# Quadrant matmuls, contiguous PSUM copies and six early expert units in a metaformer block

## The reference, cut to what matters

```python
x_dct = einsum('bchw,kw->bchk', x, MW); x_dct = einsum('bchw,kh->bckw', x_dct, MH)   # 2D DCT of each 64x64 plane
x_tri = windows of 8x8 frequencies, [4, 64, 64, 16]
q, k  = l2norm(split(x_tri @ Wq)), l2norm(split(x_tri @ Wk));  v = split(x_tri @ Wv)
attn  = softmax(einsum('bnhdm,bnhem->bnhde', q, k) * rescale)                        # channel attention, 4 heads
x_low = (attn @ v) @ proj_w + proj_b
h1    = gelu(conv3x3_depthwise(gelu(conv1x1(x_dct))))
x_conv = h1 + x_dct
x_high = gelu(conv1x1(x_conv)) + x_conv
mixed  = coef * x_low + (1 - coef) * x_high + x_dct       # with a weight per frequency
x1     = x + inverse 2D DCT(mixed)
out    = x1 + sum over 8 experts of gate_e * (gelu(layernorm(x1) @ W1_e + b1_e) @ W2_e + b2_e)   # gates: top 2 of 8
```

## Time and profile before

| | us |
|---|---|
| median of three executions (228.82 to 233.05) | 229.17 |
| span of the profiled execution, first to last instruction | 227.4 |
| median less span | 1.8 |

### The profile page before, as it was taken

How to read it: one execution, slowest core, us unless ns; L and a number is a source line. 1 busy time by engine, 2 the same in 40 slices (tenths; PEclk the granted TensorE clock), 3 DMA queues, 4 the chain that set the end, 5 groups by cost and what they waited for, 6 DMA issues and landing times.

```text
span 227.4 us, 4913 instructions
## 1 busy us (share of the span) xinstructions
PE 206.7 (91%) x2096; PEld 113.6 (50%) x2096; DVE 123.8 (54%) x232; ACT 128.1 (56%) x207; POOL 47.0 (21%) x50
## 2 busy tenths in 40 slices
PE   7699788999976898988899799999999999999993
PEld 3395667566334577963524244444444444444430
DVE  0582055659949977999731633554334553334555
ACT  2256942035338553669685387666786666786640
POOL 5560393040069992030400000000000000000000
PEclk9979999999999999999699999999999999999998
DMA  6990000000000000000005953260804508063001
GB/s 219 294 265 14 0 3 6 3 0 7 0 0 4 0 3 0 3 0 0 3 0 164 220 128 69 82 151 0 184 3 108 122 4 184 0 150 84 0 0 46
DMA packets 6596, 14.35 MB, mean 63 GB/s; under 512 B 2736, under 2 KB 4144, under 8 KB 5680
## 3 DMA queue, kind: packets, MB, share of 16 engines
q1 hardware_dynamic: 6576, 14.06, 24.7%
HBM read 12.87 MB, written 1.18 MB: 62 GB/s over the span
## 4 chain that ended last, share of the span: by engine, by line
PE 68%; ACT 9%; DMA 7%; POOL 6%; DVE 6%; SPq 1%; issue 1%; POOLq 1%; DVEq 0%
PE psum L710 22%; PE psum L694 21%; PE psum L538 7%; DMA xs<-in_x 3%; DMA wide<-gate_store 2%; PE psum L512 2%; POOL place L920 2%; ACT place L747 2%; PE psum L634 2%; PE psum L548 2%; PE psum L424 2%; POOL place L926 2%; ACT hid L861 1%; POOL place L919 1%; PE psum L557 1%
## 5 line engine op out<-in xcount | busy, mean ns | idle before, releaser
L694 PE MATMUL psum<-tok,w1s 128*64 128x512 f16 x512 | 60.8, 383 | 1.3 <-ACT hid L861 0.8
L1160 DVE SCALAR_TENSOR_TENSOR term<-psum,sm,wide 128x512 f32<-128x512 f32 x32 | 24.0, 750 | 62.1 <-PE psum L710 51.6
L861 ACT ACTIVATE hid<-psum,b1p 128x512 f32<-128x512 f32 x64 | 38.2, 701 | 16.7 <-PE psum L694 16.3
L694 PEld LDWEIGHTS psum<-tok,w1s 128*64 128x64 f16 x512 | 28.7, 110 | 35.9 <-issue 9.1
L861 ACT ACTIVATE w1f<-psum,b1p 128x512 f32<-128x512 f32 x32 | 19.6, 688 | 17.1 <-PE psum L694 17.0
L710 PE MATMUL psum<-hid,w 128*64 128x512 f32 x128 | 28.9, 593 | 0.0
L1165 DVE TENSOR_TENSOR x<-x,term 128x512 f32<-128x512 f32 x32 | 22.1, 692 | 1.1
L861 ACT ACTIVATE w1g<-psum,b1p 128x512 f32<-128x512 f32 x32 | 19.7, 714 | 0.2
L710 PEld LDWEIGHTS psum<-hid,w 128*64 128x64 f32 x128 | 9.1, 137 | 15.1 <-issue 9.4
L710 PE MATMUL psum<-w1g,w 128*64 128x512 f32 x64 | 15.1, 594 | 1.4 <-DVE term L1160 1.4
L538 PE MATMUL psum<-h_pad,tap_bd 64*64 64x512 f32 x144 | 15.9, 589 | 0.0
(11 more groups left out here) (147 smaller groups left out, 295.4 us busy)
## 6 DMA issues: line engine op xcount, KB each, us to landing
wide<-gate_store SPq DMA_DIRECT2D x14, 512.0 KB, 6.4
xs<-in_x SPq DMA_DIRECT2D x2, 512.0 KB, 5.6
w1f<-in_W SPq DMA_DIRECT2D x2, 512.0 KB, 10.0
block_out<-x SPq DMA_DIRECT2D x4, 256.0 KB, 6.4
wide<-gate_store SPq DMA_DIRECT2D x2, 384.0 KB, 5.1
...
```

The lines of the kernel that those rows point to most:

```text
L694: mm = pe.matmul(h_bank(n)[side * H:(side + 1) * H, :], w1s[:, part, e, k * P + side * H:k * P + (side + 1) * H], tok[:, pair, half, b, :] ...
L861: act.activation(hid_of[u % 4][:, t, :], h_bank(n), ACT.Gelu, bias=b1p[:, e * KT + k:e * KT + k + 1]).then_inc(gelu_ready, 1)
L1160: dve.scalar_tensor_tensor(term[:, u % 2, :], y_bank(u), b2t[:, e:e + 1], gate_b[part][:, e % (E // 2), :], ALU.add, ALU.mult).then_inc(te ...
```

## The change

- **Quadrants.** Every 128x128 matmul of the DCTs, of `tokens`, and of the router becomes four 64x64 matmuls, one for each quadrant of the array (`quarters()` lists 32 of them for a stage), and the constants shrink to one 64x64 matrix. The transposes become 64x64 matmuls with an identity (`half_ident`).
- **Contiguous copies.** The copies from PSUM no longer rearrange. `dct_over_w` and `windows` write PSUM with a stride of 8 elements instead; `to_frequencies` and `inverse_over_kh` read their stationary operand from SBUF with a stride (8 and 16 elements).
- **Six shared copies.** For dw, xd, xt, yt, back and half ACT copies bank 0 and DVE bank 1 (`other_dw` and so on, L1032 to 1062 after). A stage now signals once, at its end, instead of once per bank.
- **POOL.** `high` has two operations per bank (L974, 975 after). A new stage `rest_ahead` (L967, 968 after) makes x_conv * (1 - coef) + x_dct, two operations per bank, before h2 is there. The constant 1 - coef moves from DVE to POOL.
- **Units.** Six units are upped early, in twelve half units at turns of their own (`UPS`), two downs and their additions come early too (`DOWNS`, `ADDS`); all later rounds stand behind turn 1000.
- **Order.** The table has new numbers for nearly all stages; the input of pair 1 is loaded ahead of the larger constants; `biases` moves ahead in DVE's order; the gates of pair 0 go out early, and gate rows are stored in pieces of 64.

```diff
-    "join": (2, 3), "high": (4, 5), "gram_matrices": (10, 16), ...
+    "join": (2, 4), "rest_ahead": (3, 6), "high": (5, 7), "gram_matrices": (12, 15), ...
...
-AHEAD = 2
+SHARED = {"dw": (1, 1), "xd": (1, 1), "xt": (1, 1), "yt": (1, 1), "back": (1, 1), "half": (1, 1)}
+EARLY, EARLY_DOWN = 6, 2
+UPS = (45, 46, 48, 49, 51, 53, 54, 55, 56, 57, 59, 62)
+DOWNS = (50, 58)
+ROUNDS = (UNITS - EARLY_DOWN) // 2
+LATE = 1000
...
+        def quarters():
+            return [(chunk, side, half) for chunk in range(CP) for side in range(2) for half in range(2)]
+        def by_side(chunk, side):
+            return slice(side * CHUNK + chunk * H, side * CHUNK + (chunk + 1) * H)
+        by_half = by_side
+        def phase(v, b, k2):
+            return bank(v, b).rearrange("p (n k) -> p k n", k=K)[:, k2]
...
             sp.dma_start(xs[:, 0, :], xv[0]).then_inc(x_in[0], 16)
+            sp.dma_start(xs[:, 1, :], xv[1]).then_inc(x_in[1], 16)
             sp.dma_start(c32[:, P:CONST_N], const32[:, P:CONST_N]).then_inc(const_in, 16)
             sp.dma_start(sm[:, :], small).then_inc(weights_in, 16)
-            sp.dma_start(xs[:, 1, :], xv[1]).then_inc(x_in[1], 16)
...
             def dct_over_w(p):
-                    mm = pe.matmul(slot(p, 1)[:, cp * P:(cp + 1) * P], dh[p][:, cp * P:(cp + 1) * P], dct_w, start=True, stop=True)
+                for cp, b, side in quarters():
+                    to = bank(slot(p, 1), side).rearrange("p (m c) -> p c m", c=CP)[rows_of(b), cp]
+                    mm = pe.matmul(to, dh[p][rows_of(side), by_half(cp, b)], dct_w[rows_of(side)], start=True, stop=True)
+                mm.then_inc(dct_w_done, 1)
             def windows(p):
-                    mm = pe.transpose(slot(p, 0)[:, k2 * P:(k2 + 1) * P], dw[p][:, k2 * P:(k2 + 1) * P], ident)
+                for k2, side, b in quarters():
+                    mm = pe.matmul(phase(slot(p, 0), b, k2)[rows_of(side)],
+                                      dw[p][rows_of(b), by_side(k2, side)], half_ident[rows_of(b)], start=True, stop=True)
...
             def to_frequencies(p):
-                    mm = pe.transpose(slot(p, 1)[:, k2 * P:(k2 + 1) * P], x_out[p][:, k2 * P:(k2 + 1) * P], ident)
+                    mm = pe.matmul(bank(slot(p, 1), side)[rows_of(b), k2 * H:(k2 + 1) * H],
+                                      phase(x_out[p], b, k2)[rows_of(side)], half_ident[rows_of(side)], start=True, stop=True)
             def inverse_over_kh(p):
-                    mm = pe.matmul(slot(p, 0)[:, cp * P:(cp + 1) * P], back[p][:, cp * P:(cp + 1) * P], idct_h, start=True, stop=True)
+                of_channel = back[p].rearrange("p (m c) -> p c m", c=C)
+                    mm = pe.matmul(slot(p, 0)[rows_of(side), by_half(cp, b)], of_channel[rows_of(b), side * CP + cp], idct_h[rows_of(b)],
+                                   start=True, stop=True)
...
+            def rest_ahead(p):
+                pool.wait_ge(xconv_ready, p + 1)
                 pool.wait_ge(coef_ready, 1)
                 for b in range(B2):
+                    link(pool.tensor_tensor(bank(rest[p], b), bank(x_conv[p], b), coef_rest[:, :], ALU.mult))
+                    link(pool.tensor_tensor(bank(rest[p], b), bank(rest[p], b), bank(xd[p], b), ALU.add))
+            def high(p):
+                for b in range(B2):
                     pool.wait_ge(h2_ready, 2 * p + b + 1)
-                    link(pool.tensor_tensor(bank(h2[p], b), bank(h2[p], b), bank(x_conv[p], b), ALU.add))
                     link(pool.tensor_tensor(bank(h2[p], b), bank(h2[p], b), coef_rest[:, :], ALU.mult))
-                    pool.tensor_tensor(bank(rest[p], b), bank(h2[p], b), bank(xd[p], b), ALU.add).then_inc(rest_ready, 1)
+                    pool.tensor_tensor(bank(rest[p], b), bank(h2[p], b), bank(rest[p], b), ALU.add).then_inc(rest_ready, 1)
...
             def keep_xd(p):
-                for j in range(2):
-                    act.wait_ge(xd_done, 2 * p + j + 1)
-                    act.copy(xd[p].rearrange("p (n k) -> p k n", k=K)[:, 4 * j:4 * j + 4],
-                             bank(slot(p, 0), j).rearrange("p (k n) -> p k n", n=P)).then_inc(xd_ready, 1)
+                act.wait_ge(xd_done, p + 1)
+                for j in banks("xd", p):
+                    act.copy(bank(xd[p], j), bank(slot(p, 0), j)).then_inc(xd_ready, 1)
...
+            def other_xd(p):
+                if SHARED["xd"][p]:
+                    dve.wait_ge(xd_done, p + 1)
+                    dve.tensor_copy(bank(xd[p], 1), bank(slot(p, 0), 1)).then_inc(xd_other, 1)
...
             def mix_branches(p):
                 for b in range(B2):
                     dve.wait_ge(low_done, 2 * p + b + 1)
+                    link(dve.scalar_tensor_tensor(bank(low_term[p], b), bank(slot(p, 1), b), weight("proj_b"), coef, ALU.add, ALU.mult))
                     dve.wait_ge(rest_ready, 2 * p + b + 1)
+                    dve.tensor_tensor(bank(x_out[p], b), bank(low_term[p], b), bank(rest[p], b), ALU.add).then_inc(xout_ready, 1)
```

373 lines of the change are left out of this document (197 added, 176 removed).

## The result

The changed kernel takes 238.78 us (median of 4 runs, 236.14 to 239.96) against 229.64 for the kernel before in the same comparison. The ratio is 1.0379, 95% interval 1.0332 to 1.0426: slower by 3.8%, 9 us. The profiled execution took 238.4 with a span of 236.5.

The account below looks back on a forecast made before the run. PE bounds the kernel from 118.05 on, before that ACT and a ring of dependencies of two pairs. Span 222.2, plus 3.0 for strides and 2.0 for clock, is 227.2; with 1.8 to the median 229.0, range 225 to 232 (all cases 217 to 236.5).

Parts of the forecast that it names:

- PE's list: PE from `windows` of pair 0 to end of `taps` of pair 1: 38.9 plus 0.5 of waits, instead of 46.0.
- the start: `norm_columns` of pair 1 directly follows pair 0's, so `windows` of pair 0 begins at 16.5 instead of 17.31.
- The knot: Ahead of the second `join`: `inverse_norms`, `softmax_in`, `exponent` delay `gelu_depthwise` of pair 1; `join` at 62.4 instead of 64.48.
- the collision: DVE and POOL take turns reading two SBUF operands; `rest_ahead` beside `inverse_norms` of pair 1 costs DVE about 4.4.
- POOL to x_out: From the second `join`, 13 POOL operations take 22.05, to 84.45; x_out of pair 1 at 85.2.
- Pair 0's path: `project` of pair 1 precedes `times_wv` of pair 0; softmax ready about 71, low about 78, tokens at 88.5.
- Strides: Eight matmul stages with a strided side, each nothing to one us longer, at most some 5 on the path; +3.0 taken.
- Clock: Two idle gaps of PE in the knot lower its granted clock, each costing 0 to 2; +2.0 taken.
- Early stage: First up to late rounds: ACT's gelus set the pace, eight more at 0.685 make it 22.2 instead of 16.4.
- Late rounds: PE's remaining 13 rounds of ups and 15 of downs take 96.3; downs end at 218.1 instead of 223.3.
- the slower one: Rival: strided matmuls bind, each of the eight stages 2 us longer or more, time beyond 233.8; chance 0.24.

Follow-up runs that it names:

- the run with ACT's own copy: The changed kernel with ACT alone copying both halves of dw of pair 0: 239.25 us, ratio 1.0355.
- The late rest: The changed kernel with POOL's `rest_ahead` of pair 0 behind the `join` of pair 1: 233.43 us, ratio 1.0152.
- the old order: Changed kernel with the earlier kernel's order from `gram_times_w` on, POOL's old list, copies on ACT alone: 237.33 us; with `biases` moved into a DVE pause 233.43 us.

## Why the prediction was wrong

The forecast was no change, 229.0, with a range to 236.5; the profiled execution took 238.4, 9.4 more. Three steps failed: PE's list, whose waits were taken for gone; the start; and, the largest, the path from the second `join` to the tokens, which was put through POOL and runs through DVE's line. By the steps:

- *Start: wrong.* Put at 16.5, measured 18.95. DVE's first squares came at 7.51 instead of 6.4, and `other_dw`, behind the `norm_columns` of pair 1, at 18.12. +2.45. Traces of kernels with the same start lie between 16.8 and 19.8, none as early as the forecast; what the 2.45 are worth at the end the run with ACT's own copy could not tell.
- *PE's list: wrong.* 38.9 of work and 0.5 of waits against 39.96 and 3.07 in the window from 18.95 to 61.98. The waits were taken for gone with the order; 2.6 of the new ones are marked "issue", in four pieces of which the 1.08 at 38.34 is the longest. +3.6.
- *The knot: right in the collision, wrong in what it holds up.* `inverse_norms` of pair 1 9.6 (52.23 to 61.8; put at 8.8), `gelu_depthwise` of pair 1 6.0 us behind its taps (put at 5.4), the join at 69.23, later than 62.4 by 0.8 more than the two steps above. The late rest shows what the collision costs: 5 us, the largest single cause. But the forecast let it cost through ACT and the join, and with the join 8.3 earlier nothing was won: it costs through DVE's line. Its reading of the earlier trace rows was off as well: L1036 took 0.69 while POOL was at work (from 64.48 without rest); what sets its row apart from that of L1040 is the PSUM operand.
- *POOL to x_out: wrong path.* From the second `join` to POOL's end 19.5 (put at 22.05), but `mix_branches` of pair 1 begins only 5.1 after that end, when `low` is there (93.87). Pair 0's path was underrated: low at 86.6 is 17.3 after the join (put at 15.6), the tokens 32.4 after it (put at 26.1). +6.3, the largest miss: DVE's second softmax, `project` and `times_wv` stand one behind the other, and `to_frequencies` of both pairs wait for it. Why these stages need as much even without the collision (6.1 more than before from `windows` to the tokens) stays open; the old order did not bring it back.
- *Strides: right in size for reads, wrong for writes, and not seen as a price.* +3.0 was taken: a us for each reading stage, half a us for each writing one, half of that on the path. (1.14 over 8 steps is 142 ns, not 134, and the bound 1.1 a stage.) Writes cost nothing: `dct_over_w` takes 1.15 with them, the unstrided `tokens` 1.15. Reads cost the full upper bound, 2.0 to 2.2 instead of 1.16, but the changed kernel's runs can't tell it (under 2 us), and with the late rest it was nothing. The Trainium skill, "PSUM — Partial Sum Buffer", Specifications (TRN2), has any non-contiguous pattern slow matmuls significantly; the trace disagrees for an fp32 write with a stride of 8 elements (1.15 with it and without).
- *Clock: right in size in the trace* (3.75 for 1.95, 2.59 for 1.6), *not seen as a price before the tokens*: with gaps filled, that stretch and the time stayed. Behind the wait for pair 1's gates it can cost 1.6 to 2.9, which the forecast did not have.
- *Early stage: right in number, in part by luck.* 22.6 for 22.2, but 1.91 of it is PE's wait for the gates of pair 1, which the forecast did not have; it gave the stage to ACT's gelus. *Late rounds: right*, 96.4 for 96.3; they begin at 135.7, not at 120 to 127, as all before them is late.

The sum of the misses at the join is 2.45 + 3.6 + 0.8 = 6.85; with 6.3 behind it, less the 5.0 held for strides and clock, 8.15 at the tokens; 0.4 each in the way to the first up and in the early stage make 9.0 of the 9.4; 0.4 lies in the late rounds and behind the last `down`.

Of the rivals, the slower one had the right sign for another reason: its strided reads came near to doubling, but they explain 2.6 us at most, and in the changed kernel less than its runs can tell. The collision, the largest cause shown, stood in the forecast itself, and was priced as a loss of what was won instead of as a loss below it.
